# Routed experts on sorted token lists instead of dense tiles, in a two-layer decoder

## The chip, the cores and the metric

The kernel runs on one core of one Trainium2 chip. The metric is the device time of one execution in microseconds, the lower the better; three runs are shown, and their median is the time quoted.

## The reference

The program is a two-layer decoder on 4 x 256 tokens of width 256 (T = 1024). Layer 0 is windowed attention, cross attention and a mixture of experts; layer 1 is attention, a retention block and a memory layer. The change is in the mixture of experts of layer 0:

```python
shared = einsum('ti,hi->th', silu(x @ sh_gate_w.T) * (x @ sh_up_w.T), sh_down_w)      # inner width 704
probs = softmax(x @ router_weight.T)                                                  # 8 experts
top_v, top_i = top_k(probs, 2); top_v = top_v / top_v.sum(-1)
combine = (one_hot(top_i, 8) * top_v[..., None]).sum(1)
for e in range(8):                                                                    # inner width 176 each
    gate, up = split(x @ gate_up_proj[e].T)
    out += (silu(gate) * up @ down_proj[e].T) * combine[:, e:e + 1]
out += sigmoid(x @ shared_gate_w.T) * shared
```

Each token uses two of the eight experts. All arithmetic is float32; x is the normed row, and out is added to the residual.

## The kernel before

The stages run one after the other, each a block with one program for each engine; engines meet only through semaphores, and each engine and each DMA queue works in its written order. `experts_0` (L1364) treats all experts as one dense layer of inner width 8 x 176 + 704 = 2112, cut into 17 tiles of 128 (`M0_TILES`). For a tile n, `gate_up(n)` on TensorE makes gate and up products for all 1024 tokens in two halves of 512 (banks pg and pu). Each product of float32 operands is `split_product` (L139): both operands are cut into a high and a low F32R part, and three products are added. ScalarE takes SiLU (`silus`, L1523), VectorE multiplies by up (`times_up`, L1622) and then by the weight of the token's expert (`times_combine`, L1632), ScalarE and VectorE cut the result hT into high and low parts, and `down(n)` adds 24 products of 256 columns to four accumulator banks acc that stay open over all tiles. TensorE's order is gate_up(n), down(n - 1), so VectorE and ScalarE work on one tile while TensorE has the next.

Routing runs beside gate_up(0): the logits come from a plain F32 product (L1664), VectorE finds the two largest and builds comb, the weight of each token for each of 13 column groups; TensorE turns it (L1698), it goes through DRAM (few, table), and SP's queue loads for each tile a [128, 1024] tile cw of weights spread over the partitions, beside the tile's own gate/up and down weights. GpSimd has, after the norm's root, only the low parts of the next stage's first weights (L1490).

At the end VectorE adds acc to the residual x (L1647), takes the row statistics (L192, L195), GpSimd takes the roots, and `attention_1` (L1718) begins: VectorE scales the rows, TensorE turns them (L252), 32 warm-up products (`keep_busy`, L153) follow, then the first head's projections. `attention_1` loads each head's weights with SP while the head before is computed. The weights of attention_1, retention_1 (x1) and memory_1 (f1) that are needed first are fetched by SP during `cross_attention_0` (L1031).

## Time and profile before

| | us |
|---|---|
| median of 3 runs | 1054.7 |
| the three runs | 1051.37, 1054.7, 2532.23 |
| span of the profiled execution, core 0 | 1051.0 |
| the stage of the experts (first transposes of x to the first ones of attention_1) | 413.9 to 579.0 |
| its dense tiles, TensorE | 423.2 to 573.6 |

The page gives the span of the profiled execution, from its first to its last instruction, and no time around it. Each time in the tables and rows is in us from the start of that span unless marked ns. A matmul's length contains the latency of the pipeline, so the pace of TensorE is read from the distance of starts, not from lengths.

### The profile page before, as it was taken

The numbers are of one execution on the slowest core, as the hardware profiler recorded it, in microseconds if no ns is written. First come the engines' busy times: TensorE is split into PE (matmuls) and PEld (weight loads), VectorE is DVE, ScalarE is ACT, GpSimd is POOL, SyncE is SP. The second block draws the span as 40 slices with busy tenths as digits, with TensorE's granted clock in tenths as the row PEclk, the third lists the DMA queues.
The fourth block names the chain that finished last, engine by engine and source line by source line (L and its number), as shares of the span: only waits on it lengthen the run. The fifth ranks groups of instructions, "written<-read, shape, count | busy, mean of one in ns | idle before, by whom it ended". The sixth has DMA issues, their size and how long they took to land. (4 is left out here: it accounts for less than half of the span.)

```text
span 1051.0 us, 21544 instructions
## 1 busy us (share of the span) xinstructions
PE 1001.9 (95%) x7288; PEld 834.8 (79%) x7288; DVE 739.5 (70%) x2177; ACT 625.5 (60%) x1562; POOL 376.0 (36%) x366
## 2 busy tenths in 40 slices
PE   8899999999998998999999899999999998989988
PEld 6677778777776556888888689888989896778877
DVE  7677777777764577555556577777778786569984
ACT  2177777777783773333433777778777775334433
POOL 5866767676654012000002543444444341010000
PEclk9999999999999999999999999999999999999999
DMA  5361222111004100365441001010101000001111
GB/s 178 71 193 27 47 56 57 37 37 41 2 2 180 40 2 11 82 156 109 108 100 26 26 17 37 19 36 25 40 15 40 25 12 1 1 1 46 46 33 55
DMA packets 26125, 53.41 MB, mean 51 GB/s; under 512 B 4258, under 2 KB 11554, under 8 KB 24766
## 3 DMA queue, kind: packets, MB, share of 16 engines
q1 hardware_dynamic: 26046, 52.39, 19.0%
q8 instruction: 45, 0.74, 0.3%
q14 instruction: 34, 0.28, 0.1%
HBM read 42.30 MB, written 1.69 MB: 42 GB/s over the span
## 5 line engine op out<-in xcount | busy, mean ns | idle before, releaser
L524 ACT ACTIVATE sb_a_P<-sb_a_nS,sb_a_nm 128x257 f32<-128x257 f32 x256 | 127.6, 507 | 86.3 <-DVE sb_a_nm L635 86.0
L434 POOL TENSOR_TENSOR sb_a_P<-sb_a_P,sb_a_rec 128x512 f32<-128x512 f32 x128 | 129.2, 1040 | 87.6 <-DVE sb_a_rec L646 87.5
L635 DVE CUSTOM_DVE_ANT_0 sb_a_nS<-a_pS,sb_a_mask,sb_a_nsink 128x256 f32<-128x256 f32 x256 | 109.2, 477 | 38.8 <-PE a_pS L783 38.8
L1962 ACT ACTIVATE sb_a_t<-a_pp,sb_a_w 64x512 f32<-64x512 f32 x128 | 87.4, 683 | 14.0 <-PE a_pp L143 6.1
L2034 DVE SCALAR_TENSOR_TENSOR sb_a_t<-a_pp,sb_a_w,sb_a_cs 128x512 f32<-128x512 f32 x64 | 47.7, 745 | 57.0 <-ACT sb_a_t L1962 57.0
L143 PE MATMUL a_pp<-sb_x_high,sb_a_w_low 128*128 128x512 f32 x184 | 78.4, 426 | 6.7 <-DVE sb_a_P L590 3.8
L1886 POOL TENSOR_TENSOR sb_a_qT<-sb_a_t 128x512 f32<-128x512 f32 x32 | 41.2, 1289 | 108.4 <-DVE sb_a_t L2037 108.4
L143 PE MATMUL a_pp<-sb_x_high,sb_a_w_high 128*128 128x512 f32 x184 | 73.0, 397 | 0.0
L143 PE MATMUL a_pp<-sb_x_low,sb_a_w_high 128*128 128x512 f32 x184 | 72.6, 395 | 0.0
L533 ACT COPY sb_xn<-a_pT 128x512 f32<-128x512 f32 x128 | 67.9, 583 | 1.9 <-PE a_pT L797 1.9
L797 PE MATMUL a_pT<-sb_ident,sb_a_P 128*128 128x128 f32 x512 | 68.2, 276 | 0.3 <-ACT sb_xn L533 0.3
L797 PEld LDWEIGHTS a_pT<-sb_ident,sb_a_P 128*128 128x128 f32 x512 | 56.2, 141 | 13.0 <-issue 13.0
L783 PE MATMUL a_pS<-sb_a_kr,sb_a_qT 32*128 32x256 f32 x1024 | 65.0, 391 | 0.0
L807 PE MATMUL a_pOY<-sb_xn,sb_a_v 128*64 128x256 f32 x512 | 62.8, 386 | 0.8 <-ACT sb_xn L533 0.8
L1622 DVE TENSOR_TENSOR sb_m_hu<-sb_m_sg,m_pu 128x512 f32<-128x512 f32 x34 | 23.3, 687 | 54.9 <-ACT sb_m_sg L1523 54.9
L2078 DVE SCALAR_TENSOR_TENSOR sb_x<-a_pY,sb_a_rec,sb_x 128x256 f32<-128x256 f32 x128 | 54.8, 469 | 3.3 <-PE a_pY L2197 3.3
L783 PEld LDWEIGHTS a_pS<-sb_a_kr,sb_a_qT 32*128 32x128 f32 x1024 | 49.8, 187 | 8.4 <-issue 6.1
L1886 POOL TENSOR_TENSOR sb_a_kT<-sb_a_t 128x512 f32<-128x512 f32 x32 | 41.2, 1288 | 40.0 <-DVE sb_a_t L2037 40.0
L1523 ACT ACTIVATE sb_m_sg<-m_pg 128x512 f32<-128x512 f32 x34 | 20.2, 597 | 59.3 <-PE m_pu L143 59.3
L1490 POOL TENSOR_TENSOR sb_a_w_low<-sb_a_w,sb_a_w_high 128x512 fp32r<-128x512 f32 x2 | 2.7, 1331 | 146.6 <-ACT sb_a_w_high L131 146.6
L807 PEld LDWEIGHTS a_pOY<-sb_xn,sb_a_v 128*64 128x64 f32 x512 | 34.0, 136 | 25.4 <-issue 9.7
L524 ACT ACTIVATION_READ_ACCUMULATOR sb_a_P<-sb_a_nS,sb_a_nm 128x1 f32 x256 | 49.4, 193 | 0.0
(424 smaller groups left out, 3132.7 us busy)
## 6 DMA issues: line engine op xcount, KB each, us to landing
sb_m_cw<-m_table SPq DMA_DIRECT2D x15, 512.0 KB
sb_a_kr<-sb_a_kall SPq DMA_DIRECT2D x28, 256.0 KB, 4.0
sb_f_w<-f_w SPq DMA_DIRECT2D x12, 384.0 KB, 3.1
sb_m_gu<-m_gu SPq DMA_DIRECT2D x17, 256.0 KB, 6.3
sb_a_w<-a_w SPq DMA_DIRECT2D x16, 257.0 KB, 2.7
sb_m_dn<-m_dn SPq DMA_DIRECT2D x17, 128.0 KB, 7.0
sb_a_w<-a_w SPq DMA_DIRECT2D x8, 259.0 KB, 2.7
sb_a_wo<-a_wo SPq DMA_DIRECT2D x8, 256.0 KB, 2.7
```

What stands on the lines that cost most here:

```text
L143: ins = nc.tensor.matmul(out, a[p], b[q], start=start and i == 0, stop=stop and i == 2, **kw)
L434: nc.gpsimd.tensor_tensor(part, part, rec[b % 2][:, h, :].rearrange("p (q o) -> p q o", o=1) .to_broadcast([P, 2, S]), ALU.mult).then_inc( ...
L524: out = nc.scalar.activation(Pm[b % 2][:, h, qt, 0:S + 1], nS[:, h, qt, 0:S + 1], ACT.Exp, bias=nm[b % 2][:, h, qt:qt + 1], scale=-1.0, ac ...
L533: nc.scalar.copy(PT[h], pT[h % 2][:, :]).then_inc(PT_ready, 1)
L635: out = nc.vector.tensor_tensor_reduce(nS[:, h, qt, 0:S], pS[h][:, qt * S:(qt + 1) * S], wmask[:, qt, :], -1.0, nsink[par][:, h:h + 1], AL ...
L783: out = nc.tensor.matmul(pS[h][:, qt * S:(qt + 1) * S], qT[par][e][strip, c:c + P], kr[par][e][strip, b * S:(b + 1) * S], start=(e == 0), ...
L797: out = nc.tensor.transpose(pT[h % 2][:, (2 * c + qt) * P:(2 * c + qt + 1) * P], Pm[b % 2][:, h, qt, c * P:(c + 1) * P], k.tile["ident"][: ...
L807: out = nc.tensor.matmul(pOY[h * A0_D:(h + 1) * A0_D, p * S:(p + 1) * S], values_at(G, 2 * b + c), PT[2 * p + h][:, c * S:(c + 1) * S], st ...
L1886: nc.gpsimd.tensor_tensor(dst[:, half * NC:(half + 1) * NC], t1[c % 2][:, :, :].rearrange("p b s -> p (b s)"), t2[c % 2][:, :, :].rearrang ...
L1962: out = nc.scalar.activation(t2[n][a, :, :].rearrange("p b s -> p (b s)"), pp[n][b, :], ACT.Identity, bias=bias[b])
L2034: nc.vector.scalar_tensor_tensor(out=t1[n][:, :, :], in0=pp[n][:, :].rearrange("p (b s) -> p b s", b=2), scalar=bias, in1=table(0), op0=AL ...
L2078: out = nc.vector.scalar_tensor_tensor(out=k.x[:, 2 * u + c, :], in0=pY[:, c * D:(c + 1) * D], scalar=rec[u][:, c:c + 1], in1=k.x[:, 2 * u ...
```

## The change

The dense tiles now hold the shared expert alone (704 = 6 tiles, `M0_TILES`). The routed experts work on lists. Routing gives for each token its two experts; counting matmuls against a triangle and a matrix of ones give each (token, expert) its rank, and VectorE turns these into positions in a list sorted by expert, each expert's part rounded up to whole tiles of 128 rows: 23 slots (`M0_SLOTS`), whatever the routing. GpSimd scatters each token's normed row, with its first expert's number and its own number in two more columns (`M0_ROW` = 258), twice into a DRAM tensor by 16 indirect DMAs of 128 rows. That tensor has been filled in the stage before by a DRAM to DRAM copy with blank rows. SP loads the rows of two slots at a time (a pair, 12 of them, the last with one slot) into a ring of three buffers. For a slot TensorE turns the rows, makes gate and up products (128 x 352) with the expert's weights, which are all resident (4.3 MB loaded at the stage's head) and are addressed by the expert's number, read into a register by `value_load`; ScalarE takes SiLU, VectorE multiplies, TensorE turns the result and makes the down product (128 x 256), VectorE copies it, and GpSimd scatters it by indirect DMA into a DRAM tensor y of 2 x 1024 rows and as many dump rows as there are slots. All of that is plain F32, not split.

TensorE's order: four dense gate_ups (`M0_FRONT`), the pairs in a software pipeline, the last two dense tiles. At the end SP reads y back (4 DMAs, 2 MB) over xn and xT, and VectorE adds it with the tokens' weights, then acc with the shared gate's weight. The fetch of x1 and f1 moves from cross_attention_0 to attention_1's SP program, behind `w_of(2, 0)`; retention_1 clears the semaphores a little differently.

```diff
-    "m0": [("m0_rw", [P, KD, 9], F32), ("m0_iota", [P, 8], F32)]
+    "m0": [("m0_rw", [P, KD, 9], F32), ("m0_consts", [P, 112], F32), ("m0_tri", [P, 2, P], F32)]
...
-            k.fetch(sp, src, "a1", "x1", "f1")
+            k.fetch(sp, src, "a1")
+            sp.dma_start(k.sorted_rows, src["m0_blank"]).then_inc(k.blank_in, 16)
...
-M0_GRAN = 16
-M0_PER = M0_I // M0_GRAN
-M0_TILES = -(-(M0_E * M0_I + M0_SH) // P)
-M0_COLS = -(-M0_TILES * P // M0_I)
+M0_TILES = -(-M0_SH // P)
+M0_FRONT = 4
+M0_IH = M0_I // 2
+M0_EW = 2 * M0_I
+M0_SLOTS = 2 * T // P + M0_E - 1
+M0_ROW = D + 2
+M0_RING = 3
...
+            gate_up_of(2)
+            for d in range(KD):
+                sp.dma_start(egu[d][:, :], src["m0_egu"][d]).then_inc(egu_in, 16)
+            gate_up_of(3)
+            down_of(2)
+            for c in range(2):
+                sp.dma_start(edn[c][:, :], src["m0_edn"][c]).then_inc(edn_in, 16)
+            gate_up_of(4)
+            down_of(3)
+            sp.wait_ge(sent, 16 * 2 * NT)
+            for j in range(M0_RING):
+                rows_of(j)
+            gate_up_of(5)
+            down_of(4)
+            down_of(5)
+            for j in range(M0_RING, PAIRS):
+                rows_of(j)
+            for j in (PAIRS - 2, PAIRS - 1):
+                sp.wait_ge(y_out[j % 2], y_sent(j))
+            for half in range(2):
+                for c in range(2):
+                    rows = y_rows[c * T + half * NC:c * T + (half + 1) * NC].rearrange("(t p) n -> p t n", p=P)
+                    sp.dma_start(y[c][:, half * HALF:(half + 1) * HALF, :], rows).then_inc(y_in[half], 16)
...
+            pool.wait_ge(k.blank_in, 16)
+            pool.wait_ge(tagged, 2)
+            pool.wait_ge(placed, 1)
+            for t in range(NT):
+                for c in range(2):
+                    nc.gpsimd.indirect_dma_start(sorted_rows, bass.IndirectOffsetOnAxis(pos[:, 2 * t + c:2 * t + c + 1], 0),
+                                                 k.xr[:, t, :], None).then_inc(sent, 16)
+            for j in range(PAIRS):
+                pool.wait_ge(named, j + 1)
+                pool.wait_ge(y_ready, j + 1)
+                for s in slots_of(j):
+                    nc.gpsimd.indirect_dma_start(y_rows, bass.IndirectOffsetOnAxis(row[j % 4][:, s:s + 1], 0),
+                                                 yb[j % 2][:, s, :], None).then_inc(y_out[j % 2], 16)
...
+            for n in range(M0_TILES):
+                if n == M0_FRONT:
+                    for j in range(PAIRS):
+                        silu_of_pair(j)
+                        if j + 1 < PAIRS:
+                            turned_rows(j + 1)
+                if 0 < n < LAST:
+                    gate_up_high(n + 1)
+                elif n == LAST:
                     first_weights_high()
...
+                silus(n)
+                if n == M0_FRONT - 1:
+                    turned_rows(0)
+                down_high(n)
+                h_high_of(n)
...
+            dve.wait_ge(counted, 1)
+            total = acc[1][:, NT * M0_E:(NT + 1) * M0_E]
+            nc.vector.tensor_tensor(over[:, :, :], total.rearrange("p (e o) -> p e o", o=1).to_broadcast([P, M0_E, M0_E]),
+                                    steps.rearrange("p (o e) -> p o e", o=1).to_broadcast([P, M0_E, M0_E]),
+                                    ALU.is_gt).then_inc(ranked, 1)
...
+            nc.vector.tensor_copy(pos[:, :], posf[:, :]).then_inc(placed, 1)
...
+            def name_pair(j):
+                n = len(slots_of(j))
+                rows = xg[j % M0_RING]
+                dve.wait_ge(xg_in[j % M0_RING], 16 * (j // M0_RING + 1))
+                nc.vector.tensor_tensor(other[:, 0:n], rows[:, 0:n, D], owner[:, 2 * j:2 * j + n], ALU.not_equal)\
+                    .then_inc(rows_named, 1)
+                dve.wait_ge(rows_named, j + 1)
+                nc.vector.scalar_tensor_tensor(out=row[j % 4][:, 0:n], in0=other[:, 0:n], scalar=float(T),
+                                               in1=rows[:, 0:n, D + 1], op0=ALU.mult, op1=ALU.add).then_inc(named, 1)
+            def up_of_pair(j):
+                n = len(slots_of(j))
+                dve.wait_ge(x_silu, j + 1)
+                if j > 0:
+                    dve.wait_ge(h_turned, j)
+                nc.vector.tensor_tensor(hx[:, 0:n, :], sx[:, 0:n, :], pg2[:, 0:n, M0_I:2 * M0_I], ALU.mult).then_inc(x_up, 1)
+            def turned_pair(j):
+                n = len(slots_of(j))
+                dve.wait_ge(h_turned, j + 1)
+                if j >= 2:
+                    dve.wait_ge(x_down, j - 1)
+                nc.vector.tensor_copy(hgT[j % 2][:, 0:n, :, :].rearrange("p s c q -> p (s c q)"), pu[0][0:M0_IH, 0:n * D])\
+                    .then_inc(hgT_ready, 1)
+            def products_of_pair(j):
+                n = len(slots_of(j))
+                dve.wait_ge(x_down, j + 1)
+                if j >= 2:
+                    dve.wait_ge(y_out[j % 2], y_sent(j - 2))
+                nc.vector.tensor_copy(yb[j % 2][:, 0:n, :].rearrange("p s n -> p (s n)"), pu[1][:, 0:n * D])\
+                    .then_inc(y_ready, 1)
...
+            for n in range(M0_TILES):
+                if n == M0_FRONT:
+                    for j in range(PAIRS + 1):
+                        if j > 0:
+                            turned_pair(j - 1)
+                        if j < PAIRS:
+                            name_pair(j)
+                            up_of_pair(j)
+                        if j > 0:
+                            products_of_pair(j - 1)
+                if 0 < n < LAST:
+                    gate_up_low(n + 1)
+                times_up(n)
+                down_low(n)
+                h_low(n)
+            dve.wait_ge(share_ready, 4)
             for half in range(2):
...
+                tiles = range(half * HALF, (half + 1) * HALF)
+                dve.wait_ge(y_in[half], 32)
+                for c, s in ((0, 0), (1, 2)):
+                    for i, t in enumerate(tiles):
+                        if c == 1:
+                            dve.wait_ge(y_added, 2 * half * HALF + i + 1)
+                        nc.vector.scalar_tensor_tensor(out=k.x[:, t, :], in0=y[c][:, t, :], scalar=share[:, t, s:s + 1],
+                                                       in1=k.x[:, t, :], op0=ALU.mult, op1=ALU.add).then_inc(y_added, 1)
+            for half in range(2):
+                for t in range(half * HALF, (half + 1) * HALF):
+                    dve.wait_ge(summed, t // 2 + 1)
+                    dve.wait_ge(y_added, (half + 1) * 2 * HALF)
+                    nc.vector.scalar_tensor_tensor(out=k.x[:, t, :], in0=acc[t // 2][:, (t % 2) * D:(t % 2 + 1) * D],
+                                                   scalar=share[:, t, 1:2], in1=k.x[:, t, :], op0=ALU.mult, op1=ALU.add)\
+                        .then_inc(added, 1)
...
+                        if between and h == 0 and off == 0:
+                            between()
+                            pe.wait_ge(hgT_ready, PAIRS)
+                        if between and h == 1 and off == 0:
+                            pe.wait_ge(y_ready, PAIRS)
...
+            def turn_pair(j):
+                pe.wait_ge(xg_in[j % M0_RING], 16 * (j // M0_RING + 1))
+                if j == 0:
+                    pe.wait_ge(h_ready, 2 * M0_FRONT - 1)
+                if j >= 1:
+                    pe.wait_ge(xgT_ready, j)
+                if j >= 2:
+                    pe.wait_ge(hgT_ready, j - 1)
+                for s in slots_of(j):
+                    for d in range(KD):
+                        out = nc.tensor.transpose(pu[0][:, (s * KD + d) * P:(s * KD + d + 1) * P],
+                                                  xg[j % M0_RING][:, s, d * P:(d + 1) * P], k.tile["ident"][:, :])
+                out.then_inc(xg_turned, 1)
+            def gate_up_of_pair(j):
+                pe.wait_ge(xgT_ready, j + 1)
+                if j == 0:
+                    pe.wait_ge(h_ready, 2 * M0_FRONT)
+                    pe.wait_ge(egu_in, 16 * KD)
+                    pe.wait_ge(owned, 2)
+                else:
+                    pe.wait_ge(x_up, j)
+                for s in slots_of(j):
+                    e = expert_of(j, s)
+                    for d in range(KD):
+                        out = nc.tensor.matmul(pg[s][:, 0:M0_EW], xgT[j % 2][:, s, d, :],
+                                               egu[d][:, bass.ds(e * M0_EW, M0_EW)], start=(d == 0), stop=(d == KD - 1))
+                out.then_inc(x_gated, 1)
+            def turn_hidden(j):
+                pe.wait_ge(x_up, j + 1)
+                pe.wait_ge(xgT_ready, min(j + 2, PAIRS))
+                for s in slots_of(j):
+                    for c in range(2):
+                        out = nc.tensor.transpose(pu[0][0:M0_IH, (s * 2 + c) * P:(s * 2 + c + 1) * P],
+                                                  hx[:, s, c * M0_IH:(c + 1) * M0_IH], k.tile["ident"][:, :])
+                out.then_inc(h_turned, 1)
+            def down_of_pair(j):
+                pe.wait_ge(hgT_ready, j + 1)
+                if j == 0:
+                    pe.wait_ge(edn_in, 32)
+                else:
+                    pe.wait_ge(y_ready, j)
+                for s in slots_of(j):
+                    e = expert_of(j, s)
+                    for c in range(2):
+                        out = nc.tensor.matmul(pu[1][:, s * D:(s + 1) * D], hgT[j % 2][:, s, c, :],
+                                               edn[c][:, bass.ds(e * D, D)], start=(c == 0), stop=(c == 1))
+                out.then_inc(x_down, 1)
+            def expert_of(j, s):
+                i = 2 * j + s
+                return pe.value_load(expert[0:1, i:i + 1], min_val=0, max_val=M0_E - 1)
...
+            gate_up(0)
             pe.wait_ge(lg_ready, 1)
             pe.wait_ge(zero_set, 1)
             for a in range(4):
-                nc.tensor.matmul(acc[a][:, :], zeros[:, 0:P], zeros[:, :], start=True, stop=False, skip_group_check=True)
-            gate_up(1, 1)
-            down(0, 0)
-            with pe.Fori(0, PAIRS) as i:
-                for s in range(2):
-                    gate_up(i * 2 + (2 + s), s)
-                    down(i * 2 + (1 + s), 1 - s)
-            gate_up(LAST, LAST % 2)
-            down(LAST - 1, 1 - LAST % 2)
-            down(LAST, LAST % 2, last=True)
+                clear(a)
+            pe.wait_ge(hot_ready, 4)
+            nc.tensor.matmul(acc[1][:, 0:NT * M0_E], tri, both[:, :, :].rearrange("p t e -> p (t e)"),
+                             start=False, stop=False, skip_group_check=True)
+            for t in range(NT):
+                out = nc.tensor.matmul(acc[1][:, (t + 1) * M0_E:(NT + 1) * M0_E].rearrange("p (t e) -> p t e", e=M0_E), ones,
+                                       both[:, t:t + 1, :].to_broadcast([P, NT - t, M0_E]),
+                                       start=False, stop=(t == NT - 1), skip_group_check=True)
+            out.then_inc(counted, 1)
+            gate_up(1)
+            pe.wait_ge(ranked, 5)
+            clear(1)
+            down(0)
+            for n in range(2, M0_FRONT):
+                gate_up(n)
+                if n == M0_FRONT - 1:
+                    turn_pair(0)
+                down(n - 1)
+            gate_up_of_pair(0)
+            turn_pair(1)
+            down(M0_FRONT - 1)
+            for j in range(1, PAIRS):
+                turn_hidden(j - 1)
+                gate_up_of_pair(j)
+                if j + 1 < PAIRS:
+                    turn_pair(j + 1)
+                down_of_pair(j - 1)
+            turn_hidden(PAIRS - 1)
+            gate_up(M0_FRONT, between=lambda: down_of_pair(PAIRS - 1))
+            for n in range(M0_FRONT + 1, M0_TILES):
+                gate_up(n)
+                down(n - 1)
+            down(LAST, last=True)
...
+            k.fetch(sp, src, "x1", "f1")
...
```

## Rows read from the trace of the kernel before

**Rows 1.** Busy time by engine, the page: us, share of the span, instructions.

```profile
PE 1001.9 (95%) x7288; PEld 834.8 (79%) x7288; DVE 739.5 (70%) x2177; ACT 625.5 (60%) x1562; POOL 376.0 (36%) x366
```

**Rows 2.** Busy time by stage: window, its length, each engine, clock, DMA share, GB/s.

```profile
440.00:572.00 132.00, 131.22 (x757) 114.78 (x756) 75.41 (x129) 52.26 (x98) 4.57 (x4) 1.00 0.46 102
...
440.00:447.80 7.80, 7.80 (x47) 6.80 (x46) 5.98 (x11) 3.40 (x7) 0.00 (x0) 1.00 0.52 79
```

**Rows 3.** Timeline of TensorE around one dense tile: start, length, instruction.

```profile
558.22 0.28 PE L143 MATMUL m_acc<-sb_m_dn_high,sb_m_h_low 128*128 128x256 f32 x1
...
561.09 0.40 PE L143 MATMUL m_pg<-sb_x_high,sb_m_gu_low 128*128 128x512 f32 x1
...
566.68 0.28 PE L143 MATMUL m_acc<-sb_m_dn_high,sb_m_h_low 128*128 128x256 f32 x1
```

**Rows 4.** Waits in the stage: who waited for whom, total, times, longest.

```profile
POOL sb_a_w_low L1490 <- ACT sb_a_w_high L131: 146.6, 1, 146.6
...
PE m_acc L143 <- DVE sb_m_h_low L136: 2.0, 2, 1.3
```

**Rows 5.** Two lines with plain F32 products: instructions, ns, first and last start.

```profile
L2409 PE MATMUL x_ba<-sb_xT,sb_x_wh x8: 592/592/697, 895.4 to 898.5; 128*128 128x512 f32 x8
...
L2444 PE MATMUL x_ba<-sb_x_V,sb_x_A x32: 379/379/379, 907.6 to 914.3; 128*128 128x256 f32 x32
```

**Rows 6.** Timeline of TensorE, warm-up products of the next stage.

```profile
581.58 3.74 PE L153 MATMUL a_pY<-sb_ident 128*128 128x128 f32 x32
```

**Rows 7.** Groups of VectorE by line: count, busy us, mean ns, idle before.

```profile
L1622 DVE TENSOR_TENSOR sb_m_hu<-sb_m_sg,m_pu 128x512 f32<-128x512 f32 x34 | 23.3, 687 | 54.9 <-ACT sb_m_sg L1523 54.9
...
L2078 DVE SCALAR_TENSOR_TENSOR sb_x<-a_pY,sb_a_rec,sb_x 128x256 f32<-128x256 f32 x128 | 54.8, 469 | 3.3 <-PE a_pY L2197 3.3
```

**Rows 8.** Register move, DMA issues and landings, and the two GpSimd sizes.

```profile
L1841 SPq MOVE sb_a_wv<-a_wv x6: 29/29/29, 599.1 to 790.6; - x6
...
L1442 SPq DMA_DIRECT2D sb_m_gu<-m_gu x15: 328/333/374, 417.7 to 537.7; - x15
...
sb_a_wo<-a_wo SPq DMA_DIRECT2D x16, 128.0 KB, 2.0
...
sb_ctxT<-ctxT SPq DMA_DIRECT2D x1, 1024.0 KB, 5.0
...
L1886 POOL TENSOR_TENSOR sb_a_kT<-sb_a_t 128x512 f32<-128x512 f32 x32 | 41.2, 1288 | 40.0 <-DVE sb_a_t L2037 40.0
...
L406 POOL TENSOR_TENSOR sb_a_wv_low<-sb_xT,sb_a_wv_high 128x1024 fp32r<-128x1024 f32 x1 | 2.4, 2393 | 2.2 <-ACT sb_a_wv_high L131 2.2
```

**Rows 9.** Timeline of the head of the stage.

```profile
425.92 0.36 DVE L1595 TENSOR_TENSOR sb_m_hot<-sb_m_iota,sb_m_atf 128x64 f32<-128x64 f32 x2
...
428.70 0.40 PE L143 MATMUL m_pu<-sb_x_high,sb_m_gu_high 128*128 128x512 f32 x1
...
429.14 0.60 ACT L1523 ACTIVATE sb_m_sg<-m_pg 128x512 f32<-128x512 f32 x1 [1.17 <-PE m_pu L143]
...
431.82 1.03 PE L1705 MATMUL m_acc<-sb_m_zeros 128*128 128x512 bf16 x4
...
432.50 0.58 PE L143 MATMUL m_pg<-sb_x_high,sb_m_gu_low 128*128 128x512 f32 x1
```

**Rows 10.** Busy time in the head, columns as in rows 2.

```profile
432.60:440.00 7.40, 6.14 (x28) 4.71 (x27) 2.68 (x5) 1.96 (x4) 0.00 (x0) 1.00 0.77 190
```

**Rows 11.** Timeline of the tail and of the next stage's first transpose; last down product.

```profile
L143 PE MATMUL m_acc<-sb_m_dn_high,sb_m_h_high x136: 278/283/283, 440.0 to 573.3; 128*128 128x256 f32 x136
...
577.38 0.38 DVE L195 BATCH_NORM_AGGREGATE sb_mv<-sb_stats 128x2 f32<-128x6 f32 x4
...
578.97 0.30 PE L252 MATMUL a_pS<-sb_ident,sb_xn 128*128 128x128 f32 x1 [0.92 <-DVE sb_xn L2013]
```

**Rows 12.** The value weights of the next stage: their load and their GpSimd reader.

```profile
L1841 SPq DMA_DIRECT2D sb_a_wv<-a_wv x7: 332/333/343, 599.1 to 826.4; - x7
...
L1874 POOL TENSOR_TENSOR sb_a_wv_low<-sb_a_wv,sb_a_wv_high x7: 1268/1272/1275, 625.3 to 841.4; 128x512 fp32r<-128x512 f32 x7
```

369 lines of the change are left out of this document (196 added, 173 removed).

## The prediction

> **What bounds the kernel now.** Read the page first: TensorE is busy 95% of the span [rows 1]. The change sits in one stage, so cut the span there. In the table by stages, TensorE is busy 131.2 of the 132 us from 440 to 572, the run of dense tiles, at clock 1.00; VectorE has 75, ScalarE 52, GpSimd 5 [rows 2]. Nothing but TensorE's own stream ends last in that stretch. One tile is read off three starts: down 558.22 to 561.09 = 2.87 us, gate and up 561.09 to 566.68 = 5.59 us [rows 3], together 8.46. So time comes back only as TensorE leaves work out, unless its queue is then made to wait; GpSimd's 146.6 us of idling [rows 4] show that the scatter's engine is free.
>
> **What goes.** 17 tiles become 6: 11 × 8.46 = 93.1 us of TensorE.
>
> **What the sorted lists add on TensorE.** Their products are plain F32. Such a call is two instructions: the line with four calls of 512 columns has 8, from 895.4 to 898.5, so 3.1/7 = 0.443 us each; the one of 256 columns has 32, 6.7/31 = 0.216 each [rows 5]. A call so costs 0.89 us for 512 columns, 0.43 for 256, and for 352 by columns 0.61. A transpose is about 0.12, as the 128-column warm-up products are: 32 took 3.74 us [rows 6]. A slot is 2 gate/up products (1.22), 2 down (0.86), 4 transposes (0.46) = 2.54 us; 23 slots 58.4 us.
>
> Can a pair run at 5.08 us? After its products the next step needs SiLU and up: ScalarE has 0.60 and VectorE 0.69 for 512 columns [rows 7, 9], so for 352 about 0.5 + 0.55, and 0.2 for handing over, about 1.3 us, while TensorE has the next transposes and the previous down products, 2.2 us. VectorE has per pair 0.52 + two copies of 0.68 + two small operations, 2.2 us; ScalarE 1.1. All are hidden, with 0.9 us of slack.
>
> **The register loads.** Each slot reads its expert's number into a TensorE register twice: 46 loads that no row shows. Bounds: a register move is 0.03 us; a whole DMA lands after 2.0 [rows 8]. At four a pair that is 0.1 to 8 us beside 5.08 of work, so 0 to 3 us a pair exposed, 0 to 33 in all; below nothing is excluded, it is added work. I take 2 us, since TensorE's queue is fed ahead and the nearer row is the move. The Trainium skill (DMA: Bandwidth & Descriptors, Latency and other measured facts) gives a tensor_load a floor of about 0.6 us, which would be 2.4 us a pair, still under the products: the sum would stay.
>
> **The head.** The combine transposes, their warm-up matmuls and the wait for the first weights row go; counting and ranking come. Before, gate_up(0) issues its last product at 428.7 and gate_up(1) starts at 432.5 [rows 9]. After: clears 0.85 (four, 1.03 busy), nine counting calls (18 instructions of at most 64 columns at about 0.09) 1.6: 431.4. Then VectorE runs 9 small operations to `placed`, 4 more for the owners and 4 for the shares, at about 0.18 each (two took 0.36) [rows 9], a little more where 184 columns or a wait stand between: placed 433.5, all at 435.4. **Here a wait is moved:** times_up(0) is queued behind them on VectorE, and gate_up(1) waits for its first half: start 436.1, 3.6 us late. The old stall ahead of the first down (1.3) [rows 4] and the shorter hT chain give back about 1.4. TensorE idles 4.7 us here.
>
> **Scatter against the front.** Dense tiles 1 to 3 then cover it: 436.1 + 3 × 5.59 + 2 × 2.87 + 0.2 = 458.8, where turn_pair(0) needs the sorted rows. GpSimd issues 16 indirect DMAs of 128 rows from 433.5. No row shows one. Bounds: 0.33 us, the issue of a plain one on SP's queue; 2.4 us, GpSimd's longest tensor operation [rows 8]. I take 1.3, its 128x512 operation, the commonest of its rows and inside both ends. 16 × 1.3 = 20.8: 454.3, landing 2.5: 456.8, read back 3.2: 460.0, so a stall of 1.2 us; at 0.33 none, at 2.4 a stall of 18.8. SP's queue holds 4.3 MB of expert weights ahead of that; at the 190 GB/s that the busiest part of the head reached [rows 10], 23 us of the 40 available, and gu(3) behind the first 2.9 MB arrives near 435, needed at 450: nothing. GpSimd's 2 scatters per pair (2.6 us) hide in 5.08; SP's read of 264 KB has two pairs' time.
>
> **The end.** TensorE ends at 458.8 + 1.2 + 9.1 (down(2), down(3), the first pair's gate/up 2.44, 8 transposes) + 54.2 (10 steps of 5.08 and one of 3.4, which has a single slot) + 2 (loads) + 18.0 (2 × 5.59 + 2 × 2.87 and the last slot's 1.1) = 543.3. Before it was 573.6. But VectorE now owes 16 additions of y at 0.44 (a 256 column three-operand operation is 0.47 busy), and 8 in place of 4 from PSUM [rows 7, 11]. The last y rows leave TensorE at about 528, are in DRAM at 532; 2 MB read back, at 5.0 us for 1 MB [rows 8], come at 538 and 543. VectorE is free of h_low at 541; additions until 547.8; then 2 × 3.5 for PSUM additions and statistics: 554.8. Before, statistics ended at 577.8 and the first transpose of the next stage began 1.2 us later at 579.0 [rows 11]: now 556.0. **23.0 us won**, where TensorE alone would have given 30.
>
> TensorE idles from about 546 to 556 and for 4.7 us in the head. The granted clock stayed 1.00 with waits of at most 1.3 us [rows 2, 4], so no row prices this. At 1.2 instead of 2.4 GHz the 32 warm-up matmuls, 3.74 us [rows 6], take 3.7 more; bounds 0 and 7 us over both places, I take 3. The Trainium skill (TensorE: Matmul & The Clock Gate, HAM oscillation) says that idle gaps drop the clock and that work after them starts slow; by it part of this is paid.
>
> **Moved fetches.** x1 and f1 (2.8 MB, 13 issues, about 6 us of SP) leave the cross attention's stage and come behind w_of(2,0) in attention_1; the 3 MB blank copy takes their place, where nothing waits for the queue. Behind them is wv(1), issued at 599.15 and used by GpSimd, behind a 0.6 us cast, at 625.3 [rows 12]: 6 us of issue and 15 of transfer leave it at about 622. I take 0; bounds 0 and 5. The xn row of 258 columns and the wider constants: nothing, same operations.
>
> **Sum.** 1051.0 − 23.0 + 3 = 1031 in the profiled execution; the page gives its span alone, nothing around it, and the median shown is 3.7 above it, the fastest run 0.4. Between these: **1034 us** against 1054.7. A measurement here tells 2% (21 us) from no change; the forecast lies just there.
>
> **Rivals.**
> 1. **GpSimd becomes the bound (slower).** If a scatter costs its longest operation and one VectorE operation that it waits out, 2.4 + 0.7 = 3.1 us: sorted rows at 488.8, stall 30, less the 1.2; the pairs at 6.2 instead of 5.08, + 12; tail + 3. + 44: 1078. The gain is gone near 2.5 us a scatter, and 2% slower is reached near 3.1. For it: VectorE is busy 5.98 of 7.80 us, 77%, in such a tile's time [rows 2]. Against: GpSimd's 512-column operations stay 1.3 us beside a busy VectorE. Chance 0.10. The Trainium skill (SBUF — State Buffer, Who interferes with whom) lets VectorE's two-input operations hold off GpSimd's reads, and its box on DMAs issued there gives 3.1 us for one of 0.62; no run here shows either.
> 2. **The pair is bound by latency.** Register loads near 1.5 us, or a chain of GU, SiLU, up, transpose that doesn't close within the 0.9 us of slack: 6.3 us a pair, + 14: 1048. For it: every step is single-buffered (sx, hx, pg). Against: row by row it fits. Chance 0.25.
> 3. **All added costs hide**: scatter under 1.2, loads free, clock held: − 6 and the y reads earlier by 4: 1024. Chance 0.17.
> 4. **Mixed misses**, scatter near 2 us with late weights in attention_1: + 12 + 5: 1052. Chance 0.08.
> That the work is not cut is no rival: 6 tiles and 23 slots are fixed in the loops, whatever the routing.
>
> The forecast has 0.40. Its own range is 1024 to 1043, so half of it is over 2% faster (below 1033.6), with rival 3: faster 0.38; slower than 1075.8 only rival 1 and a corner of 2: 0.09; the rest 0.53. Range: rival 3 down to 1016 (head wait and tail shorter as well) and up to 1062, the scatter's upper bound with rival 2's half; rival 1 is left out.
>
> **What would show it.** PE's instructions in the stage; starts of the first transposes of xg and what they wait for (1.2 us, or more if the scatter is dear); GpSimd's mean per indirect DMA, 1.3; distance of two pairs, 5.1 to 5.3; gate_up(1) starting 7 us after gate_up(0) ends, released by VectorE; TensorE idle about 10 us ahead of attention_1 with VectorE on y. Wrong it is if a pair takes 6 us or more, if the stall before the pairs is over 8 us, or if the clock falls for longer than the two places.

## The result, and where the time went

The changed kernel takes **1038.3 us** (four runs, 1036.4 to 1040.6) beside 1053.9 for the kernel before: ratio 0.985, 95% interval 0.983 to 0.987. (1053.9 is the median of four runs, a slow one of 2532 us among them; the three shown ahead of the prediction had 1054.7.) A second measurement of the same program, beside three of the experiments below, gave 0.982 (0.979 to 0.984). The forecast was 1034 us. So the change is faster, by 1.5 to 1.8%; the first interval leaves 2% out, the second just touches it.

In the profiled execution the span went from 1051.0 to 1034.9 us. The page's busy times, to be held against [rows 1]; the last row is the new queue of the indirect DMAs (packets, MB, share of the span of 16 DMA engines):

```profile
PE 972.2 (94%) x7027; PEld 802.5 (78%) x7029; DVE 714.2 (69%) x2168; ACT 599.7 (58%) x1518; POOL 415.3 (40%) x406
...
q0 software_dynamic: 1872, 5.13, 1.4%
```

TensorE is busy 29.7 us less (the forecast had its stream end 30.3 earlier); the span gives back only 16. Cut the stage into windows (length, each engine's busy time, clock, DMA share, GB/s), as in [rows 2, 10]:

```profile
430.00:440.00 10.00, 5.20 (x26) 4.49 (x25) 6.90 (x23) 1.75 (x4) 4.07 (x4) 0.74 0.22 53
440.00:450.00 10.00, 10.00 (x52) 8.41 (x52) 3.52 (x6) 3.09 (x6) 7.56 (x9) 0.92 0.84 238
450.00:460.00 10.00, 6.86 (x33) 5.35 (x32) 1.33 (x3) 1.96 (x5) 4.25 (x5) 0.93 0.51 168
460.00:470.00 10.00, 10.00 (x55) 8.84 (x55) 4.43 (x8) 4.14 (x9) 0.00 (x0) 0.90 0.23 70
480.00:530.00 50.00, 49.51 (x238) 37.59 (x237) 20.51 (x51) 10.07 (x21) 19.22 (x20) 1.00 0.29 86
553.00:560.00 7.00, 0.12 (x2) 0.00 (x0) 6.03 (x23) 0.00 (x0) 2.53 (x4) 0.83 0.00 0
560.00:566.00 6.00, 3.17 (x15) 3.20 (x16) 2.77 (x8) 1.13 (x2) 2.71 (x4) 0.50 0.07 22
```

Three holes are to be seen in the first number behind the length: 5.20 of 10 in the head, 6.86 of 10 at 450, and almost nothing from 553 to 562.8, each with a clock under 1.00 in it or behind it (1.00 is TensorE's 2.4 GHz, 0.50 its 1.2). The pairs, in 480 to 530, are full.

**The head** is as forecast. The timeline (start, length, instruction, in brackets the idle time and what ended it), to be held against [rows 9]:

```profile
429.96 1.90 PE L1903 MATMUL m_acc<-sb_m_both,sb_m_tri 128*128 128x64 f32 x16
433.91 0.17 DVE L1685 CAST sb_m_pos<-sb_m_posf 128x16 uint32<-128x16 f32 x1
435.01 1.23 POOL L1517 DMA_INDIRECT m_sorted<-sb_xn,sb_m_pos  x1 [17.31 <-DVE sb_m_pos L1685]
435.84 1.28 DVE L1715 TENSOR_TENSOR sb_m_hT<-sb_m_sg,m_pu 128x512 f32<-128x512 f32 x2
436.66 0.77 PE L146 MATMUL m_pg<-sb_x_high,sb_m_gu_low 128*128 128x512 f32 x1 [4.80 <-DVE sb_m_hT L1715]
```

gate_up(1) starts at 436.7 (forecast 436.1), and its products then take 0.43 us each instead of 0.23 up to 441.5: TensorE had been idle for 4.8 us and was granted 1.2 of its 2.4 GHz.

**The second hole was not forecast.** The same view from 452 on:

```profile
452.79 0.39 PE L146 MATMUL m_pu<-sb_x_low,sb_m_gu_high 128*128 128x512 f32 x1
453.63 0.48 PE L146 MATMUL m_pu<-sb_x_high,sb_m_gu_high 128*128 128x512 f32 x1 [0.45 <-issue]
455.73 0.28 PE L146 MATMUL m_acc<-sb_m_dn_low,sb_m_h_high 128*128 128x256 f32 x1 [1.51 <-issue]
456.44 0.38 PE L146 MATMUL m_acc<-sb_m_dn_high,sb_m_h_high 128*128 128x256 f32 x1 [0.43 <-issue]
457.15 1.42 SPq L1479 DMA_DIRECT2D sb_m_xg<-m_sorted  x3
457.86 0.28 PE L146 MATMUL m_acc<-sb_m_dn_low,sb_m_h_high 128*128 128x256 f32 x1 [0.42 <-issue]
458.04 0.60 ACT L1563 ACTIVATE sb_m_sg<-m_pg 128x512 f32<-128x512 f32 x1 [10.76 <-remote]
```

("remote" is what the profile writes when it finds no instruction that released the wait.) ScalarE waits 10.8 us for a product that TensorE had issued by 450.3. In the trace's record of semaphore updates TensorE's updates for down(0), and for the two halves of gate_up(2), which were due at about 447.8, 450.7 and 454.1, stand at 457.89, 458.01 and 458.14; the last landing of the scatter that is on record is at 457.13. TensorE itself crawls from 452.8 on ("issue": it waits for nothing that the profile shows), and from 458.7 to 461.2 its 256-column products start 0.21 us apart instead of 0.12, at half clock. turn_pair(0) comes at 467.3, 7.3 us behind the forecast.

**The third** is the switch to attention_1 (beside it before, [rows 11]):

```profile
562.20 0.19 POOL L182 TENSOR_SCALAR sb_a_spread<-sb_mv 128x4 f32<-128x4 f32 x1 [3.56 <-POOLq L1378]
562.27 1.88 DVE L2230 TENSOR_SCALAR sb_xn<-sb_x,sb_mv,sb_a_root 128x256 f32<-128x256 f32 x5 [3.11 <-PEq L1378]
562.83 0.45 PE L255 MATMUL a_pS<-sb_ident,sb_xn 128*128 128x128 f32 x1 [9.71 <-DVE sb_xn L2230]
```

VectorE's statistics end at 559.2, but nobody starts before 562.2. The sequencer's instructions at the line of the block show who is late (count, ns, first and last start), in the changed kernel and then in the kernel before:

```profile
L1378 POOLq DRAIN  x1: 4369/4369/4369, 557.6 to 557.6; - x1
L1378 DVEq DRAIN  x1: 17/17/17, 559.4 to 559.4; - x1
```

```profile
L1373 POOLq DRAIN  x1: 1154/1154/1154, 576.5 to 576.5; - x1
L1373 DVEq DRAIN  x1: 17/17/17, 578.0 to 578.0; - x1
```

GpSimd's drain, with which it leaves the block, takes 4.37 us and not 1.15. From the end of the statistics to the first transpose 3.67 us pass, before 1.21.

### The profile page after: what moved, and what is told of

It is laid out like the page before. It is cut to its first block and busy times, and to the rows that moved or that the text cites. A ratio compares the mean times of both kernels' runs of the same rounds, so it can differ in the third digit from the quotient of the medians.

```text
span 1034.9 us, 20928 instructions
## 1 busy us (share of the span) xinstructions
PE 972.2 (94%) x7027; PEld 802.5 (78%) x7029; DVE 714.2 (69%) x2168; ACT 599.7 (58%) x1518; POOL 415.3 (40%) x406
## 5 line engine op out<-in xcount | busy, mean ns | idle before, releaser
L2254 DVE TENSOR_TENSOR sb_a_t<-sb_a_t,sb_a_cs 128x512 f32<-128x512 f32 x64 | 46.5, 727 | 0.0
L146 PEld LDWEIGHTS a_pp<-sb_x_high,sb_a_w_low 128*128 128x128 f32 x184 | 34.7, 189 | 13.7 <-issue 5.3
L1523 POOL DMA_INDIRECT m_y<-sb_m_yb,sb_m_row x23 | 22.1, 961 | 57.7 <-DVE sb_m_yb L1748 53.9
## 6 DMA issues: line engine op xcount, KB each, us to landing
m_sorted<-m_blank SPq DMA_DIRECT2D x1, 2967.0 KB, 14.5
```

The lines of the kernel that those rows point to most:

```text
L146: ins = nc.tensor.matmul(out, a[p], b[q], start=start and i == 0, stop=stop and i == 2, **kw)
```

## The experiments

All are edits of the changed kernel; ratios are to the kernel before. For the table, times count from the start of GpSimd's 1.17 us drain just ahead of this stage (414.55 in the changed kernel), since profiles differ by 2 to 3 us up to there. "turn_pair(0)" is the first transpose of sorted rows, "pair" the first gate/up product of the first pair, "end" the start of the drain that ends the stage, "held" ScalarE's wait put down to "remote". Two things move these times by chance. In e2, e4, e5, e6 and e7 the granted clock was 0.83 in 420 to 430, in the others 1.00, which puts all behind it later: e3 and e4, whose programs are the same up to 530 us, are 1.9 us apart at the first pair. And "held" comes and goes (see below). So a row tells of an edit only beside a row with the same luck.

| kernel | ratio (95%) | turn_pair(0) | pair | end | drain, us | held, us |
|---|---|---|---|---|---|---|
| changed | 0.985 (0.983 to 0.987) | 52.8 | 56.1 | 143.0 | 4.37 | 10.8 |
| e5 again | 0.982 (0.979 to 0.984) | 52.2 | 55.5 | 142.4 | 4.37 | 10.4 |
| e1 edn late | 0.993 (0.990 to 0.996) | 60.6 | 65.6 | 152.5 | 4.37 | none |
| e2 times_up first | 0.980 (0.977 to 0.982) | 48.3 | 53.7 | 140.7 | 4.37 | none |
| e3 drain early | 0.974 (0.972 to 0.977) | 47.1 | 50.4 | 137.4 | 1.15 | none |
| e4 busy 44 | 0.980 (0.977 to 0.983) | 49.0 | 52.3 | 139.2 | 4.37 | none |
| e6 = e2+e3+e4 | 0.976 (0.974 to 0.979) | 48.1 | 53.7 | 140.8 | 1.15 | 2.3 |
| e7 = e6, front 5 | 0.978 (0.976 to 0.981) | 52.7 | 56.0 | 140.8 | 1.15 | 6.5 |
| e8 loads twice | one run: 1056.6 us | 51.4 | 54.7 | 162.6 | 4.37 | 10.7 |
| e9 = e3+e4+fill | 0.975 (0.973 to 0.978) | 46.1 | 49.5 | 136.4 | 1.15 | none |
| e10 = e9, edn early | 0.977 (0.974 to 0.979) | 45.8 | 49.2 | 136.1 | 1.15 | none |
| e11 front done | 0.975 (0.973 to 0.978) | 46.2 | 48.7 | 134.4 | 1.16 | none |
| e12 adds on GpSimd | 0.977 (0.975 to 0.980) | 50.8 | 53.0 | 138.5 | 1.15 | 2.4 |

### e1: the routed down weights behind the sorted rows

```
-            for c in range(2): ... edn ...; gate_up_of(4); down_of(3)
             sp.wait_ge(sent, 16 * 2 * NT)
             for j in range(M0_RING): rows_of(j)
+            down_of(3); for c in range(2): ... edn ...; gate_up_of(4)
```

> Edit: the two loads of the routed down weights (edn), gate_up_of(4) and down_of(3) are issued behind the first three fetches of sorted rows instead of ahead of the scatter. In the changed kernel TensorE stood almost still from 452.8 to 458.0 us (down(1), gaps of 0.3 to 1.5 us ended by nothing in the trace) and ScalarE from 447.3 to 458.0, while the 16 DMA engines were busy 84 to 98% with these loads and the scatter. Theory A (the loads beside the scatter fill the DMA engines, and what the other engines need of them comes late): the gap at 453 to 458 is under 1 us, the scatter's last row lands before 456, span 5 to 7 us below the changed kernel's 1034.9, ratio to the kernel before about 0.979. Theory B (the scatter alone, or something tied to its end, holds TensorE): the same 5 us gap stands, ratio 0.985 as the changed kernel. Theory C (nothing but code fetched from DRAM, at that place of the program): same gap at the same place, ratio 0.985.

The hole at 453 is gone, and the kernel is some 8 us slower than the changed one (span 1043.0 for 1034.9). The waits from 456 to 480 say why (who waited for whom, total, times, longest):

```profile
ACT sb_m_gu_high L134 <- DMA sb_m_gu<-m_gu: 17.8, 1, 17.8
DVE sb_m_gu_low L139 <- ACT sb_m_gu_high L134: 17.6, 1, 17.6
```

ScalarE's queue has gate_up_high(4) ahead of silus(3), so gu(4), needed by TensorE only some 70 us later, holds the front as soon as it is late. All three theories missed this; the time says nothing of the scatter. It priced an order instead: what is behind a waiting instruction counts, and here that is the very next SiLU.

### e2: times_up(0) ahead of the ranking chain

```
+            times_up(0)
             dve.wait_ge(counted, 1)
```

(The function's definition moves up with it, and the loop further down leaves out n = 0.)

> Edit: VectorE does times_up(0) while it waits for the counting matmuls, ahead of the ranking chain, instead of behind it. Theory (the head's idle time is the order on VectorE): gate_up(1) starts within 0.5 us of the last counting matmul (431.9 us), at about 432.4 instead of 436.7, TensorE keeps its full clock there (products at 0.23 us and not 0.43), the scatter starts within 0.3 us of 435.0 as before; 4.3 us of idle time and 2.2 us of low clock go, so the dense front ends 6 us earlier. If the scatter's end (457.1) and the stall of TensorE at 453 to 458 set the time of what follows, only 0 to 1 us of that is left at turn_pair(0) and the ratio stays at 0.985; if that stall is not tied to the scatter's end, the ratio is about 0.979.

gate_up(1) starts at 432.4 with products of 0.23 us: the order on VectorE did make the head's hole. The front now ends before the rows are there. The waits from 450 to 470:

```profile
PE m_pu L1851 <- DMA sb_m_xg<-m_sorted: 6.6, 1, 6.6
```

TensorE then comes back at half clock. So what the head wins is waited out. The first pair is at 53.7: 2.4 us ahead of the changed kernel, but 1.4 behind e4, which has the changed kernel's head, no hold and the same slow clock at 420. By this comparison the new order alone wins nothing at the first pair, and the 2.4 us go rather to the hold that was absent.

### e3: a drain behind the y scatters

```
                     nc.gpsimd.indirect_dma_start(y_rows, ...)
+            nc.gpsimd.drain()
```

> Edit: GpSimd has a drain right behind its 23 y scatters, 20 us ahead of the block's end. In the changed kernel the drain that ends GpSimd's part of the block took 4.37 us (1.15 before, 1.05 of it the operation ahead of it), and all engines waited for it: the switch to attention_1 is 2.5 us longer. Theory A (the first drain behind indirect DMAs costs some 3.2 us once): the new drain takes 3 us or more, unseen beside TensorE, the last one about 1.15, the first transpose of attention_1 comes 3.0 us earlier at about 559.8, ratio about 0.982. Theory B (every drain behind indirect DMAs, or at that code address, costs it): the last drain still takes 4.4 us, ratio 0.985.

The sequencer's rows of the drains:

```profile
L1525 POOLq DRAIN  x1: 4449/4449/4449, 530.7 to 530.7; - x1
...
L1378 POOLq DRAIN  x1: 1154/1154/1154, 554.1 to 554.1; - x1
```

and in its timeline:

```profile
556.35 1.38 DVE L2231 TENSOR_SCALAR sb_xn<-sb_x,sb_mv,sb_a_root 128x256 f32<-128x256 f32 x4 [0.61 <-PEq L1378]
```

Theory A: the long drain is paid once behind the indirect DMAs, and 20 us earlier it is hidden. VectorE's wait in the switch is back at 0.61 us (0.65 before), and from the end of the statistics to the first transpose it is 1.17 us instead of 3.67, so the drain is worth 2.5 us. The ratio fell by 0.011, some 11 us. The profile shows 5.6 us more in the stage, as it has no hole at 453; what the other runs had there is not on record.

### e4: the fill at the end, 20 to 44

```
-M0_BUSY = 20
+M0_BUSY = 44
```

> Edit: M0_BUSY from 20 to 44: the fill on TensorE behind the last dense product lasts until about 559 us instead of 553.1, under the 561.9 at which GpSimd's drain ends. Theory A (TensorE idle for 9.7 us loses its clock, and the first 6 us of attention_1 pay for it): granted clock 0.9 or more in 560 to 570 instead of 0.50 and 0.67, the 32 fill products there 3.7 us instead of 4.5, the end 1 to 2 us earlier, ratio 0.983 to 0.984. Theory B (the clock falls anyway with such thin work, or the queue behind it hides it): under 0.5 us.

The dense part ended at 544.8 here, so the fill, too, was over by 554.9, 4.4 us ahead of the first transpose: the clock was 0.63 at first and not 0.50, and the 32 warm-up products took 4.24 us instead of 4.52 (3.74 at full clock, [rows 6]). From the first transpose to the first rope operation (VectorE's first step behind the first head's projections): 9.2 us before, 10.8 in the changed kernel, 10.2 here, and 9.2 in e9, e10 and e11, where the drain is early as well and 1.9 us are left between fill and first transpose. Theory A holds in its direction, with 0.6 us of the 1 to 2 that it forecast. But a short gap is not enough. e6, e7 and e12 have gaps of 1.9, 2.0 and 1.6 us, and the clock fell behind them all the same, with 10.5 to 10.6 us to the rope operation. e9 and then e6:

```profile
550.00:560.00 10.00, 8.09 (x66) 7.02 (x65) 8.30 (x24) 4.29 (x7) 4.87 (x7) 1.00 0.05 15
560.00:570.00 10.00, 9.12 (x53) 8.18 (x52) 5.21 (x12) 6.43 (x12) 0.31 (x1) 0.84 0.01 2
```

What tells the two groups apart is not known.

### e5: the changed kernel again

> Edit: none, the changed kernel a second time, beside the three below on one chip. In its first profile TensorE stood almost still from 452.8 to 458.0 us; in the runs with M0_BUSY 44 and with the earlier drain, which differ from it only behind 530 us, it did not (busy 10.0 of 10 us in 450 to 460). Theory A (the stall is chance of that execution): busy 9.5 or more of 10 us there, span 1029 to 1031, and the timed ratio, which never held it, stays at 0.985. Theory B (the stall belongs to this program's place in memory): it stands again at the same instruction, and the ratio is 0.985 with it. Theory C (it comes now and then, and was in some of the timed runs): absent here, ratio 0.980 to 0.983.

B or chance, not settled: the hole is there again, 7.65 of 10 us busy in 450 to 460, in down(1) as before, but the ratio is 0.982 and not the 0.985 of theory B.

```profile
450.00:460.00 10.00, 7.65 (x38) 5.99 (x37) 0.14 (x1) 0.77 (x2) 5.47 (x6) 1.00 0.47 166
```

### e6 and e7: everything together, with four and five tiles ahead of the pairs

```
-M0_FRONT = 4      # e7
+M0_FRONT = 5      # e7
```

> Edit: times_up(0) ahead of the ranking chain, the drain behind the y scatters and M0_BUSY 44, together; M0_FRONT stays 4. Theory A (sum of the parts, seen one by one at ratios 0.9795, 0.9744, 0.9796 against 0.9851): the drain gives 3.1 us, the clock in 560 to 570 1.5, the head 1 to 2 (TensorE then waits some 5 us for the sorted rows at turn_pair(0)), ratio 0.972 to 0.976. Theory B (the gains overlap in the same idle time): no better than the drain alone, 0.974 or above.

> Edit: as e6_front4 with M0_FRONT 5: one more dense tile (8.5 us) lies ahead of the pairs and one less behind. Theory A (the scatter's end sets turn_pair(0) once the head is quick): TensorE's wait of 7 us for the rows goes, the tail shows 2 to 3 us that down(4) no longer covers, and the y data, which then lands some 11 us behind the last pair with only 6 us of dense work behind it, sets when the y additions start, 2 to 4 us later: net 0 to 3 us better than e6_front4, ratio 0.970 to 0.975. Theory B (the tail is the longer chain): the tail gives back more than the head wins, ratio 0.976 or above.

e6 is no better than the drain alone (theory B). As in e2, TensorE waits for the rows, here 6.4 us, and comes back at half clock, so the parts overlap there; but its profile also has the slow clock at 420 and a short hold, so how much the overlap alone costs isn't shown. In e7 the fifth tile, 8.5 us, costs the front only 2.3, so it wins 6.2, and the tail gives the whole of it back: with one dense tile behind the pairs TensorE waits 3.5 us for h_low, which takes 3.44 us for its two operations beside GpSimd's where it takes 1.28 in the other kernels, and VectorE's additions start only 1.1 us earlier than in e6 (counted from the stage's start), when y has landed. The stage ends where e6's does, so by the time it is theory B, though y's landing sets the start, as theory A said:

```profile
539.60 0.55 PE L146 MATMUL m_acc<-sb_m_dn_high,sb_m_h_low 128*128 128x256 f32 x1 [3.51 <-DVE sb_m_h_low L139]
...
541.48 2.74 DVE L1777 SCALAR_TENSOR_TENSOR sb_x<-sb_xn,sb_m_share,sb_x 128x256 f32<-128x256 f32 x4 [0.34 <-DMA sb_xT<-m_y]
```

### e8: every register load twice

```
+                pe.value_load(expert[0:1, i:i + 1], ...)
                 return pe.value_load(expert[0:1, i:i + 1], ...)
```

> Edit: every expert's number is loaded into TensorE's register twice instead of once (92 loads in place of 46). Predicted before: 46 loads cost 2 us (0 to 33). Theory A (a load from SBUF is hidden behind the matmuls ahead of it): the pairs keep their pitch of 4.97 us. Theory B (a load holds the queue for 0.35 us or more, hidden only in part): the pitch grows by 4 times that, to 5.5 us or more, and the span by over 6 us.

From the first pair's first product to the last pair's last gate/up product the changed kernel has 56.5 us, this one 75.8: 19.3 more for 44 more loads, 0.44 each. The loads that the changed kernel has show no cost: its pairs run at 4.97 us, under the 5.08 that the products alone were forecast at. The rows of TensorE's sequencer in the changed kernel suggest why both are true:

```profile
L1892 PEldq TENSOR_LOAD <-sb_m_expert x46: 294/300/552, 468.9 to 531.2; - x46
L1892 PEldq FUSED_REGOPS  x46: 151/151/165, 469.5 to 531.6; - x46
```

One load and its handling hold the sequencer for 0.89 us (two loads start at 483.05 and 483.93), twice a slot 1.8 us, beside 2.5 us of products. Two loads in a row, which only e8 has, start 0.64 apart, so two more a slot are 1.3 us where 0.7 are left: 0.6 to be paid by this reckoning, 0.88 measured. Theory B in its price, theory A for what is there.

### e9, e10, e11: holding the clock, loading early, finishing the front first

```
             out.then_inc(counted, 1)
+            for _ in range(M0_HEAD):                                # 16; e9, e10
+                nc.tensor.matmul(acc[3][:, :], zeros[:, 0:P], zeros[:, :], start=False, stop=False, ...)
             gate_up(1)
```

> Edit: the early drain and M0_BUSY 44 together, and 16 matmuls that add zeros to m_acc3 in the 4.8 us in which TensorE waits for times_up(0). Theory A (that idle time is what halves TensorE's clock for the next 5 us): granted clock 1.00 in 430 to 445, the products of gate_up(1) at 0.23 us from the first on, GateUp of the first pair 2 us earlier (50.4 to 48.4 us from the start of GpSimd's drain into this block, where the drain run had 50.4 and the M0_BUSY run 52.3), ratio 0.970 to 0.973. Theory B (zeros, or so short a fill, do not hold the clock): the first pair as in the drain run, ratio 0.973 to 0.975 with the tail's gain of M0_BUSY alone.

> Edit: as e9_head_fill, and the two loads of the routed down weights are issued right behind those of the routed gate and up weights at 423 us, 15 us earlier, so that the scatter (435 to 457) runs beside two small loads alone. In three of five profiles in which these loads ran beside the scatter, TensorE's semaphore updates of 8 to 10 us reached the others only 0.7 us after the scatter's last landing (updates due at 447.7, 450.5 and 453.9 came at 457.89, 458.01 and 458.14), and 2 to 5 us were lost; in the one where they came later they did not. Theory A (the loads beside the scatter cause it): no such delay, DMA share under 0.5 in 440 to 450, the scatter lands up to 1 us earlier, ratio 0.000 to 0.002 under e9's. Theory B (the scatter alone causes it, now and then): it can show here too, ratio as e9's.

> Edit: early drain, M0_BUSY 44, times_up(0) ahead of the ranking chain, edn loads early, and down(2) and down(3) ahead of turn_pair(0) (ScalarE's copy of the turned rows behind its work for down(3)): the dense front is finished before the first sorted rows are asked for. With times_up(0) alone TensorE asked for the rows at 41 us from the block's start and got them at 48.1, then worked 3 us at half clock. Theory A (the scatter's end is the limit and the 5.8 us of down(2) and down(3) fit in front of it): turn_pair(0) at 45.5 to 48.2, the first pair's gate and up at 48 to 50.3 (53.7 with times_up(0) alone), ratio 0.969 to 0.973. Theory B (the copy and the two turns in the open, 2 us, cost what is won): first pair at 50.5 or later, ratio 0.973 or above.

e9: the clock is 1.00 through the stage, and gate_up(1) runs at speed from its second product:

```profile
433.75 1.89 PE L1910 MATMUL m_acc<-sb_m_zeros 128*128 128x512 bf16 x8
436.96 0.47 PE L146 MATMUL m_pg<-sb_x_high,sb_m_gu_low 128*128 128x512 f32 x1 [1.32 <-DVE sb_m_hT L1717]
437.27 0.39 PE L146 MATMUL m_pg<-sb_x_low,sb_m_gu_high 128*128 128x512 f32 x1
```

The first pair gains 0.9 us on e3, not 2: behind that the rows are the limit. e10 shows no hold, but neither does e9, so it doesn't decide between its theories. e11 has the earliest pair and the shortest stage, 134.4 us against 143.0, as its theory A had it, but the ratio, 0.975, is outside the 0.969 to 0.973 of that theory; TensorE finds the rows in 0.34 us of waiting and then stands 1.78 for ScalarE's copy. The timed ratios of e3, e9 and e11 are not told apart (their intervals share 0.973 to 0.977); against the changed kernel's 0.983 to 0.987 all three are better, and the intervals of e3, e6 and e9 to e12 reach to 0.980 at most, so with these edits the change is faster by over 2%.

### e12: half of the y additions on ScalarE and GpSimd

> Edit: as e11_front_done, and for the second half of the tokens ScalarE multiplies the two gathered rows by their shares and GpSimd adds them to x (8 operations each), so VectorE does 8 of the 16 y additions. Theory A (VectorE's 16 y additions at 0.40 us stand on the path to attention_1, as the prediction had it): GpSimd's drain into the switch starts 2.5 to 3.2 us earlier, at 131.2 to 131.9 us from the block's start where e11_front_done had 134.42, first transpose at 134.4 to 135.1, ratio 0.971 to 0.973. Theory B (GpSimd needs over 0.8 us an addition, or slows VectorE at the port that they share, and VectorE waits for it ahead of the second half of the shared expert's additions): the drain starts at 133.5 or later, ratio 0.974 or above.

Theory B. VectorE's first eight additions and GpSimd's eight, side by side:

```profile
541.90 2.54 DVE L1789 SCALAR_TENSOR_TENSOR sb_x<-sb_xn,sb_m_share,sb_x 128x256 f32<-128x256 f32 x4
542.50 3.31 POOL L1542 TENSOR_TENSOR sb_x<-sb_x,sb_xn 128x256 f32<-128x256 f32 x4 [2.00 <-ACT sb_xn L1626]
544.36 3.46 DVE L1789 SCALAR_TENSOR_TENSOR sb_x<-sb_xT,sb_m_share,sb_x 128x256 f32<-128x256 f32 x4
545.76 3.33 POOL L1542 TENSOR_TENSOR sb_x<-sb_x,sb_xT 128x256 f32<-128x256 f32 x4
```

Four of VectorE's take 2.54 and 3.46 us where four take 1.66 alone, so eight on VectorE last 5.9 us, nearly what sixteen last without GpSimd (6.4). From the first pair to the end of the stage it is 85.5 us, in e11 85.8: next to nothing won. The Trainium skill (SBUF — State Buffer, Who interferes with whom) says that a VectorE operation with two inputs in SBUF contends with GpSimd operations that read SBUF; the rows agree. Besides, there was a hold here: the SiLUs of gate_up(2) start at 455.7 and 458.7, for products that had ended at 452.1 and 454.9 (the profile puts only the last 2.4 us down to "remote"), and TensorE waited 3.4 us for what follows from them. The first pair came 4.4 us later than in e11, and that is why the stage as a whole is longer.

## Why the prediction was right, and where it was off

1. **What goes and what a slot costs: right.** Pairs follow each other at 4.97 us (the second, third and fourth start their gate/up products at 476.75, 481.73 and 486.70), forecast 5.08 by rows of F32 products elsewhere [rows 5, 6]. No latency shows between them, which was rival 2.
2. **Register loads: 2 us forecast, none to be seen**; e8 shows that the room beside the products is less than a second pair of loads needs. The floor of about 0.6 us in the Trainium skill (DMA: Bandwidth & Descriptors, Latency and other measured facts) is met by neither number of the changed kernel, the load alone 0.30 and one behind the other 0.89; it agrees with the 0.64 between two loads in a row in e8.
3. **The head's moved wait: right**, 4.8 us idle for 4.7, gate_up(1) 0.6 late; e2 shows the order as the cause.
4. **Scatter's price: right.** One indirect DMA is 0.96 us and 0.30 to the next, 1.27 for the 1.3 taken from the 128x512 row [rows 8]; the rows landed at 459.97, forecast 460.0. Both hits are in part luck. The 1.3 was picked between 0.33 and 2.4 from an operation that has nothing to do with a scatter; and the start was 1.5 us late (435.0 for 433.5), which the 16 issues (0.5), the landing (0.7) and the read back (0.4) gave back. GpSimd as the bound, rival 1, is out: 1.27 per slot beside 2.5. But what stood against that rival, that GpSimd's 512-column operations stay at 1.3 us beside a busy VectorE, is not always so: in e7 three of them take 1.39, 1.72 and 1.73.

```profile
L1517 POOL DMA_INDIRECT m_sorted<-sb_xn,sb_m_pos x16: 957/962/1233, 435.0 to 454.5; - x16
...
L1523 POOL DMA_INDIRECT m_y<-sb_m_yb,sb_m_row x23: 955/962/963, 482.9 to 534.3; - x23
```

5. **"So a stall of 1.2 us": the step that failed.** The scatter was priced as issue and landing alone; that other engines' work could come late while it runs was put at nothing. gate_up(2) starts at 447.7, 3.1 us late (0.6 from the head, the rest clock), and from there to turn_pair(0) 5.4 us are lost in the hole, about 1.4 of them by the slow clock behind it, where 1.2 were forecast: 467.3 instead of 460.0. TensorE did not wait for the rows at all, which had been there since 459.97.
6. **The end.** From the pairs on TensorE was 5.2 us late (2.1 came back by points 1 and 2); VectorE's y additions took 0.40 us each, forecast 0.44; the switch, forecast at the 1.2 us of before, took 3.7, by GpSimd's drain, a term that the sum did not have. So the first transpose came at 562.8 for 556.0: 16.1 us won of the 23.0. e3 shows that these 2.5 us are the drain's.
7. **Clock: forecast 3 us, measured 2.5 + 1.6** in the two places (the rope operation of attention_1 is won by 14.5), and some 1.4 in a third, behind the hole, which is counted there. So one sign of being wrong that the prediction names did come, a clock that falls for longer than the two places; the other two, a pair of 6 us and a stall over 8 us, did not. e9, e10 and e11 kept the clock in both places; e6, e7 and e12 did not at the switch.
8. **Moved fetches: 0, as forecast**: wv_low starts at 610.9, 14.4 us earlier than in [rows 12], with everything else.

The sum said 1031 for the profiled execution; it was 1034.9, and the 3 us added for a median turned out as 3.4. The mechanism was right in the main, and the error of 4 us is small by luck: 8.4 us of time that the sum lacked, less 4.6 that it had too many. It lacked two terms for which no row of before stood, 4.2 in the hole and 2.5 of drain, and besides 1.1 of clock and 0.6 in the head; it had too many in the pairs with their loads (2.1), in the additions (0.9) and, by 1.6, at the very end. That 1.6, won between the rope operation and the end, has no cause that I know; only the moved fetches and the clearing of semaphores were edited there.

**Left open: what holds the updates.** In six of thirteen profiles (changed, e5, e6, e7, e8, e12) ScalarE's wait is put to "remote", and in all six the last held update stands within 1 us of SP's first fetch of rows, which waits for the scatter. That the hold ends with the scatter is seen; that the scatter causes it is argued. It was 10.4 to 10.8 us in both profiles of the changed kernel and in e8, and absent in e3 and e4, whose instructions up to there are the same, so neither the loads beside the scatter nor the order of the front decides it. With these loads beside the scatter it came in five profiles of nine, with them early in one of three, and in e1, with them late, not at all.

One thing more sets the six apart. Their traces lack records of semaphore updates, in the time of the scatter above all: 61 to 84 of the scatter's 256 landings (16 DMAs of 16) stand in them, and in each of the seven others all 256; all records of landings are 3201 to 3229 against 3528. The instructions of the front are all there, so the late starts are real in these executions. But it is a rival that nothing here excludes: that the recording, and not the kernel, is what got stuck, or that one congestion held both. A scatter thinned out, or issued with pauses, was not tried, and no run without the recording is on record.

## What to carry to other kernels

Work taken off a saturated engine comes back only as far as the next order on the other queues allows: write for every wait that moves what stands behind it, and for a load that moves who waits for it first (e1). A producer that was hidden (here the scatter, 22 us) becomes the limit as soon as the path ahead of it is made shorter, and then improvements of that path don't add up (e2, e6, e7). GpSimd, once it has issued indirect DMAs, should be drained where nobody waits for it (e3). And a gain read from one profile is to be held against a second profile of the same program: here they differ by 2 us at the first pair through the clock alone.

## What the runs showed of the hardware

- A GpSimd drain behind indirect DMAs took 4.4 us (4.37 and 4.45) the first time and 1.15 afterwards, also when the last of them was 23 us old.
- A run's time goes with the mean granted clock of TensorE: of eleven runs of the kernel before on one chip, two at 0.998 took 1050.9 and 1051.5 us, four at 0.992 took 1056.6 to 1057.1, about 1 us for 0.001. The changed kernel was granted 0.982 to 0.988, e9 0.993 to 0.998. Part of what a change costs is in that number.
- After 4.8 us of idle time TensorE's next 5 us ran at 1.2 GHz; sixteen products with zeros put into that gap kept it at 2.4 in both kernels that had them (e9, e10).
- Beside GpSimd, VectorE's 128x256 additions took 0.64 to 0.87 us, alone 0.40 (e12); GpSimd's took 0.83, and no run has them alone. In e7 both were slowed: VectorE's subtraction for h_low took 1.72 us beside GpSimd's of 1.72, where e6 has 0.64 and 1.28.
